# Routing whole rows: tokens, gates and routing values scattered by class, expert groups loaded plainly, results added into the output

## The reference, cut to what matters

```
logits = h3 @ Wg.T                        # 8 experts
val, idx = top_k(softmax(logits), 2); val /= val.sum() + 1e-9
out = 0
for e in range(8):
    a, b = split(h3 @ W1[e].T + b1[e], 2) # 2 x 256
    out += ((a * sigmoid(b)) @ Wo.T + bo) * comb[:, e]
result = x2 + gb * out                    # gb: one row of 128 for each sequence
```

## Time and profile before

| | us |
|---|---|
| median of three runs | 815.12 (813.99 to 816.86) |
| the profiled execution | 810.64 |
| its span | 808.8 |

### The profile page before, as it was taken

One profiled execution on the slowest core, in us unless ns is written; L12 is line 12 of the kernel. 1 busy time (PEld: TensorE's weight loads), 2 busy tenths in 40 slices (PEclk: granted clock), 3 DMA queues, 4 the chain that ended last, 5 costly groups with the idle time before them and its releaser, 6 DMA issues. The chain is left out here.

```text
span 808.8 us, 14121 instructions
## 1 busy us (share of the span) xinstructions
PE 669.2 (83%) x3703; PEld 521.4 (64%) x3703; DVE 657.2 (81%) x1426; ACT 474.8 (59%) x1163; POOL 613.5 (76%) x657
## 2 busy tenths in 40 slices
PE   2566899998999789988877967329879999999993
PEld 0444577676777558665655756118668888888882
DVE  5399999999999999979999467707748887788873
ACT  3664789887997678875655655214334444444441
POOL 5377878998998688999779785636777777777763
PEclk7798999999999899998999977559989999999997
DMA  4987767887887867766774262423144433333320
GB/s 125 244 129 139 125 142 132 130 161 131 157 157 125 127 114 133 128 110 115 100 95 94 63 171 64 95 63 84 32 107 104 97 92 95 97 97 96 97 65 1
DMA packets 95298, 89.64 MB, mean 111 GB/s; under 512 B 22832, under 2 KB 71194, under 8 KB 95094
## 3 DMA queue, kind: packets, MB, share of 16 engines
q1 hardware_dynamic: 84438, 66.49, 45.0%
q0 software_dynamic: 10784, 22.25, 9.9%
HBM read 38.69 MB, written 22.41 MB: 76 GB/s over the span
## 5 line engine op out<-in xcount | busy, mean ns | idle before, releaser
L708 POOL TENSOR_TENSOR rs_prod<-rT,state 128x512 f32<-128x512 f32 x128 | 165.2, 1303 | 35.9 <-DVE state L1287 34.0
L1743 POOL DMA_INDIRECT xg<-tokens_scratch,listed x91 | 88.9, 977 | 42.0 <-issue 25.6
L1749 POOL DMA_INDIRECT out<-res,listed x91 | 91.0, 1000 | 34.6 <-issue 25.7
L1282 DVE TENSOR_TENSOR kv<-key,v_spread 128x512 f32<-128x512 f32 x128 | 84.3, 669 | 10.6 <-DMA v_spread<-vT 9.3
L1713 ACT ACTIVATE sig<-ps_a 128x256 f32<-128x256 f32 x91 | 35.0, 385 | 82.5 <-PE ps_a L1653 69.1
L1287 DVE TENSOR_TENSOR_SCAN state<-decay,state,kv 128x512 f32<-128x512 f32 x64 | 79.9, 1269 | 0.1
L1287 DVE TENSOR_TENSOR_SCAN state<-decay,kv 128x512 f32<-128x512 f32 x64 | 76.0, 1207 | 0.1
L1067 PEld LDWEIGHTS ps_k<-w,gel 128*128 128x128 f32 x512 | 61.0, 199 | 14.7 <-issue 12.5
L1715 ACT ACTIVATE sig<-ps_b 128x256 f32<-128x256 f32 x91 | 35.0, 384 | 51.5 <-PE ps_b L1653 51.5
L1067 PE MATMUL ps_k<-w,gel 128*128 128x128 f32 x512 | 64.0, 285 | 1.2 <-ACT gel L924 1.2
L1790 DVE SCALAR_TENSOR_TENSOR ps_a<-ps_a,listed,sig 128x256 f32<-128x256 f32 x91 | 44.3, 487 | 24.8 <-ACT sig L1713 24.8
(11 more groups left out here) (298 smaller groups left out, 2068.4 us busy)
## 6 DMA issues: line engine op xcount, KB each, us to landing
v_spread<-vT SPq DMA_DIRECT2D x128, 256.0 KB, 6.5
xin<-in_L_attn_x SPq DMA_DIRECT2D x16, 256.0 KB, 7.2
tokens_scratch<-mods_scratch SPq DMA_DIRECT2D x16, 256.0 KB, 10.4
x<-in_L_attn_x SPq DMA_DIRECT2D x16, 256.0 KB, 4.8
tokens_scratch<-x SPq DMA_DIRECT2D x16, 256.0 KB, 5.4
tokens_scratch<-h SPq DMA_DIRECT2D x16, 256.0 KB, 4.5
list_scratch<-gel SPq DMA_DIRECT2D x1, 3584.0 KB, 11.9
rs_prod<-in_L_ffn_W SPq DMA_DIRECT2D x8, 256.0 KB, 5.3
```

The costliest lines, as they stand in the source:

```text
L708: pool.tensor_tensor(rs_prod[:, p, idx % 4], rT[p][:], state[idx][:, p * NT:(p + 1) * NT], ALU.mult).then_inc(s["rs_ready"], 1)
L1282: dve.tensor_tensor(kv[idx % 2][:], key[:], v_spread[idx % SPREADS][:], ALU.mult).then_inc(s["kv_ready"], 1)
L1743: pool.indirect_dma_start(xg[:, 2 * (k % LOADS) + i, :], None, pay_dram, bass.IndirectOffsetOnAxis(ap=listed[:, j, ID:ID + 1].bitcast(I32) ...
L1749: pool.indirect_dma_start(out_rows, bass.IndirectOffsetOnAxis(ap=listed[:, j, ID:ID + 1].bitcast(I32), axis=0), res[k % RESULTS][:, i, :], ...
```

## The change

A row of 260 values (1040 B) now carries everything of one token: `h3`, the gate row, and the four tags. `sorted_scratch` holds 28 classes with room for all tokens and 128 rows of slack each. It replaces both scratch tensors; `tokens_scratch` keeps only `h3` of twelve tiles.

- `x2` is stored to the output itself. In the expert block the scatter adds the result onto it (`compute_op=ALU.add`), so that DVE no longer adds `x2`: `gate` and `finish` become one multiplication.
- The clearing of the list goes. One block of 128 blank rows is stored at the start, and in the expert block 28 copies of that block, DRAM to DRAM, are put behind the ends of the classes (`fill_end`), after the first 12 group loads and before the rest. The late groups wait for them.
- For two of three listed batches SP stages pairs of groups (`stage_pair`: three DMAs, `h3` from DRAM, the gate row broadcast, the tags), two pairs in each iteration; POOL scatters them from there (`list_pair`). The third batch and the late four tiles lie in `last_rows`, which takes the place of the scan states when these are done; `load_last_rows` brings the third batch's tokens (1 MB) and four gate rows, broadcast (2 MB), in iteration 20 before SP's other work, and POOL scatters all 16 groups of it at one spot.
- The second batch's listings are spread like the first's (two at each odd spot) instead of being hurried.
- In the expert block SP loads each group's rows directly to `xg`; POOL only has the 16 late listings (four in each of the first four pairs, before the scatters) and the scatters.
- `out_w_rows` is loaded in `load_experts`; a copy of the classes' ends to `end_table` stands before the late table.

```diff
-                for t, p, b in tile(4):
-                    sp.dma_start(pay_gates[t], mods_dram[b, GB:GB + 1, :].broadcast_to([NT, P])).then_inc(s["gates_stored"], 16)
+                for r in batch(3):
+                    stage_pair(r, 0)
...
+            def stage_pair(r, m):
+                if r < LISTED - 1:
+                    first, k = r * RG + 2 * m, m % 2
+                    sp.wait_ge(s["route_step"], r * Router.STEPS + Router.TAGGED)
+                    for p in range(2):
+                        sp.wait_ge(s["h3_stored"][p], 16 * BATCH // 2 * (r + 1))
+                    if r > 0 or m >= 2:
+                        sp.wait_ge(s["listed"][k], 16 * 2 * (r * RG // 4 + m // 2))
+                    sp.dma_start(stage[k][:, :, 0:P], pay_groups[:, first:first + 2, :]).then_inc(s["staged"][k], 16)
+                    sp.dma_start(stage[k][:, :, GATE:TAGS], mods_dram[first * P // (TPB * NT), GB:GB + 1, :].unsqueeze(0).broadcast_to([P, 2, P])) \
+                        .then_inc(s["staged"][k], 16)
+                    sp.dma_start(stage[k][:, :, TAGS:], tags[:, first:first + 2, :]).then_inc(s["staged"][k], 16)
+            def load_last_rows():
+                sp.wait_ge(s["rs_ready"], TILES * DK)
+                for p in range(2):
+                    sp.wait_ge(s["h3_stored"][p], 16 * (early // 2))
+                sp.dma_start(last_rows[:, 0:RG, 0:P], pay_groups[:, (LISTED - 1) * RG:, :]).then_inc(s["last_staged"], 16)
+                for i in range(2 * BATCH // TPB):
+                    first = i * TPB * NQ
+                    sp.dma_start(last_rows[:, first:first + TPB * NQ, GATE:TAGS],
+                                 mods_dram[early // TPB - BATCH // TPB + i, GB:GB + 1, :].unsqueeze(0).broadcast_to([P, TPB * NQ, P])).then_inc(s["last_staged"], 16)
...
             def list_some(r, spot):
+                if r < LISTED - 1 and spot % 2 == 1 and spot <= RG + 1:
+                    list_pair(r, spot // 2 - 1)
+                if r == LISTED - 1 and spot == 7:
+                    pool.wait_ge(s["last_staged"], 16 * (1 + 2 * BATCH // TPB))
+                    pool.wait_ge(s["tags_set"], 1)
+                    pool.wait_ge(s["route_step"], LISTED * Router.STEPS)
+                    for m in range(RG // 2):
+                        list_pair(r, m)
...
+            def load_group(j):
+                k = j // 2
+                if k >= LOADS and j % 2 == 0:
+                    sp.wait_ge(s["stored"][(k - LOADS) % RESULTS], 16 * count_to(k - LOADS, RESULTS))
+                row = sp.value_load(row_table[0:1, j:j + 1], min_val=0, max_val=CLASSES * STRIDE)
+                sp.dma_start(xg[:, slot(j), :], sorted_dram[bass.ds(row, P), :]).then_inc(s["x_in"][k % LOADS], 16)
+            def fill_end(c):
+                row = sp.value_load(end_table[0:1, c:c + 1], min_val=0, max_val=CLASSES * STRIDE)
+                sp.dma_start(sorted_dram[bass.ds(row, P), :], sorted_dram[CLASSES * STRIDE:, :]).then_inc(s["filled"], 16)
+            for j in range(2 * LOADS):
+                load_group(j)
+                if j == 1:
+                    sp.dma_start(out_b[:], ins["L0_ffn_bo"].unsqueeze(0).broadcast_to([P, P])).then_inc(s["small_in"], 16)
+            for c in range(CLASSES):
+                fill_end(c)
+            for j in range(2 * LOADS, GROUPS):
+                if j == early_groups:
+                    sp.wait_ge(s["listed"], 16 * RG)
+                    sp.wait_ge(s["filled"], 16 * CLASSES)
+                load_group(j)
...
             for k in range(PAIRS):
-                if k + AHEAD < PAIRS:
-                    gather(k + AHEAD, 0)
+                if k < LIST_AT:
+                    list_late(RG * k // LIST_AT, RG * (k + 1) // LIST_AT)
                 if k >= 1:
                     scatter(k - 1, 0)
```

More of the change, by code:

```diff
@@ L33 @@
 GATE_MIN = 0.25
-ID, LOW, HIGH, BOTH = range(4)
+ID, LOW, HIGH, BOTH, TAG = range(5)
+GATE, TAGS, ROW = P, 2 * P, 2 * P + TAG
 PACK = 1 << 12
@@ L393, in attention_block @@
         mods_early, mods_late = sb("mods_early", [P, 2, 2, P]), sb("mods_late", [P, 2, 3, P])
-        out_w_rows = sb("out_w_rows", [P, out_w.shape[1] * P])
+        stage = [sb(f"stage{i}", [P, 2, ROW]) for i in range(2)]
         setup = rs_prod[0:NROWS, 0].rearrange("p a n -> p (a n)")
@@ L698, in list_some, with list_pair @@
-            def list_some(r, spot):
-                first, end = listed_by(r, spot - 1), listed_by(r, spot)
-                if first < end:
-                    pool.wait_ge(s["route_step"], (r + 1) * Router.STEPS)
-                    pool.wait_ge(s["list_cleared"], 32)
-                for n in range(first, end):
-                    list_group(r, n)
+            pool.memset(unlisted[:, TAGS + ID:TAGS + ID + 1].bitcast(I32), TILES * NT).then_inc(s["unlisted_ready"], 1)
+            def list_pair(r, m):
+                k = m % 2
+                if r < LISTED - 1:
+                    pool.wait_ge(s["staged"][k], 48 * (r * RG // 4 + m // 2 + 1))
+                    pool.wait_ge(s["route_step"], (r + 1) * Router.STEPS)
+                for n in range(2 * m, 2 * m + 2):
+                    g = r * RG + n
+                    if r < LISTED - 1:
+                        pool.indirect_dma_start(sorted_dram, bass.IndirectOffsetOnAxis(ap=dest[:, g:g + 1], axis=0), stage[k][:, n % 2, :], None).then_inc(s["listed"][k], 16)
+                    else:
+                        pool.indirect_dma_start(sorted_dram, bass.IndirectOffsetOnAxis(ap=dest[:, g:g + 1], axis=0), last_rows[:, n, :], None).then_inc(s["last_listed"], 16)
@@ L732, in step @@
                     products(7, p)
+                    beside(t, LAST, number_last)
                 for t, p, b in tile(8):
@@ L1608, in count_to, with slot, share_of @@
             return sum(members(j) for j in range(k % ring, k + 1, ring))
-        def quad_of(j):
-            return j // LISTS if j < early_groups else LATE_QUAD + (j - early_groups) // LISTS
-        def listed_to(c):
-            return 16 * sum(quads[i][1] for i in range(c % LISTS, c + 1, LISTS))
+        def slot(j):
+            return 2 * (j // 2 % LOADS) + j % 2
+        def share_of(j, which):
+            return xg[:, slot(j), TAGS + which:TAGS + which + 1]
         block = ctx.enter_context(nc.Block())
```

192 lines of the change are left out of this document (85 added, 107 removed).

## The result

The changed kernel takes 844.23 us (842.79 to 847.24, 4 runs) against 814.56 us: ratio 1.0379, 95% interval 1.0351 to 1.0407. It is 30 us slower; 811 was forecast, with a range of 798 to 835.

A forecast was written before the change was run, and what follows sets the result against it. No one engine bounds the whole: DVE sets attention, chained small steps the drain, PE the experts except where it starves. −1 + 0 − 1.8 − 1.4 − 0.4 = −4.6 us took the median 815.1 to 811; range 798 to 835.

The forecast's parts named there:

- Start: Kernel start: without the clearing, DVE's first norm of a later tile waits less; −1 us, between 0 and −2.
- Steady iterations: Steady pipeline: removed gate broadcasts gain nothing, extra POOL work is hidden, staging fits the slack; 0, with +3 as bound.
- Rival D: Steady iterations: staging delays spread loads beyond their slack, about 2 us in each of some five iterations; 821, chance 0.06.
- Last rows: Before the drain: 3 MB queued ahead take 12 us at 263 GB/s, expert weights still come in time; 0.
- Rival B: Last rows: 2 MB of gate broadcasts go at 40 GB/s, expert weights come at 513; +22, 833, chance 0.10.
- Drain: Drain: two listings fewer gain 2.5 us, third batch's listings end about when DVE would; −1.8 us net.
- Start of the experts: Handover to experts: list load, gather and turn become one load and turn, turn 0 at 534.5; −5.8 us.
- Fills: Expert block: 28 fills at 1.1 us hold SP, so PE idles 12.9 us before turn 6.
- A: Fills cost by piece, 1.6 us each, and all loads behind them wait; 13 us added, 824, chance 0.22.
- A': Fills cost by bytes, 3.3 us each, and the loads behind them wait; +60, 871, chance 0.05.
- C: SP issues fills faster, at 0.91 us each, so the stall is 5.3 us shorter; 804, chance 0.07.
- Steady experts: Expert pairs: PE's work unchanged, 0; at the end a saved addition gives −0.4, last scatter's landing up to +2.4.

The follow-up runs named there:

- e1: Kernel before with the eight scan states in one tile, 1025 values apart, as in the changed kernel; ratio 0.9941.
- e4: Changed kernel with four gate rows of 64 KB loaded and spread by DVE instead of broadcast by DMA; 823.01 us.
- e14: Kernel before with each scan state beginning 4 bytes later in its tile, a repeat of e2; 805.88 us against 812.37, ratio 0.9933.
- e3: Changed kernel with the scan states 1032 values apart instead of 1025; 857.45 us where the kernel before took 918.71.
- e11: Changed kernel with each fill as two DMAs of 64 rows, each with its own register read; 886.71 us.
- e2: Kernel before with each scan state beginning 4 bytes later in its tile; ratio 0.9885.
- e10: Changed kernel whose scatter stores instead of adding, leaving x2 out of the result; 855.99 us where the kernel before took 915.12.

## Why the prediction was wrong, step by step

- **What bounds the kernel: half right.** PE sets the experts: pairs stay 5.27 us apart. But "DVE was busy 252.3 of 255, so DVE waited for nothing there" took busy for work. Part of that time was DVE standing behind POOL.
- **Start, −1.** Not seen: the first `h3` store is at 149.97, before at 150.16. DVE's wait of 7.20 us for `xin` is gone, and one of 9.53 us for a spread load, before 1.84, stands in its place.
- **Steady iterations, 0.** Failed: −9.3. The place of the states, which the diff shows only as a slice of a tile, is a part of it that e1 shows alone (ratio 0.9941). By e1 to e4 and e14 it is some 4 us, and 3.9 the rest, perhaps the difference between the broadcasts that left and the staging that came; this split is an estimate. The bound of +3 covered only a loss. Rival D falls: past the 9.53 us at the start DVE waits 3.5 us in all for spread loads.
- **Last rows, "12 us at 263 GB/s: 0".** The step that failed most: it priced 2 MB by the expert weights' rate although the gate row's, 40 GB/s, had the same one-row source. Measured: 25.5 us for 2 MB, 82 GB/s, between the two. And the cover was looked for in the wrong place. The prediction asked only whether the expert weights behind the load come in time. The first thing behind it that anyone needed was a staged pair, for which POOL waits, and behind POOL all else; the next was `exp_w`, for which PE waits 23.36 us and which the prediction doesn't price. Rival B had the source and the size (+22), at a chance of 0.10, and its 513 for the first product of the weights came near the 509.26 measured, but the weights were not what the drain waited for. The drain lost 35.2 in the first pair of profiles; e4 is 31.5 us shorter there than the changed kernel's first profile and 27.5 shorter than e3 on its own chip.
- **Drain, −1.8.** The two listings less are not to be seen under this. Without the broadcasts (e4) the drain is 3.7 us longer than before, and POOL waits 14.0 us for staged pairs: "where the change adds a wait, what is queued behind it" was asked of SP and not of POOL. To the first load it is 3.3 longer, not 0.6. The prediction had counted the 16 listings behind the last `h`; they took 21.6 us, not 20.3, and their rows of 1040 B landed 5.1 us behind the issue (the median of that stretch), not the 2.4 that it took from a scatter of 512 B. DVE's last table value ends 22.6 us behind the last `h`, as before (22.4), so it is by all signs the listings that the block's end now waits for.
- **Start of the experts, −5.8.** Right: −5.4, turn 0 is 4.4 us behind the first load.
- **Fills, a stall of 12.9 us.** Right in place, kind and releaser, too small in size: 19.9. A fill takes SP 1.32 us, not the 1.1 of a list load, which makes 6.2 of the 7.0 us, and lies just at the 1.3 from which the prediction had called the change slower than before. Rivals A and A' fall: the load behind the 28 fills lands in 3.2 us, and e11's half fills cost nearly as much as whole ones. C falls with the 1.32.
- **Steady experts, 0, and tail, −0.4 with +2.4 as bound.** Pairs as forecast. The last scatter is 8.1 us from the end before and 9.3 after, and comes 0.7 later behind the last turn: +1.9 from the last turn on.
- **The sum.** +36.6 where −4.6 was forecast, by the two profiles: 37.6 of the 41 are the drain, 6.7 the fills' size, 2.7 the stretch to the first load, 1.9 the tail, 0.4 the handover; the start and steady gain takes 8.3 back. In the medians it is 844.23 against a forecast of 811. The range ended at 835 because B (833) and a longer stall (A, 824) were each thought of alone.

## What to carry to other kernels

A bulk load put ahead of a queue must be priced by a row with the same source pattern, and its victims are found by walking the queue behind it instruction by instruction, through each engine that waits in order, not by asking for the one user that comes to mind. A broadcast of one DRAM row to a large tile was here better loaded once and copied by an engine that had time. Many small register-addressed DMAs cost their issue, so they go where that queue is idle, in pieces between the loads that someone needs.

## What the runs showed of the hardware that was not expected

- A POOL product of two 128x512 operands takes 1.09 us or 1.30, by where its second operand begins (period 16 bytes); 4 or 8 bytes behind the start of a tile is fast, 0 or 12 slow (all at 4: mean of 1100 ns in e2; all at 0: 1303).
- DVE's busy time contains waits behind POOL: 0.29 us of work shown as 4.07, and 5.5 us of 268 went when only POOL's products became shorter (e2, another chip).
- Four DMAs of 512 KB that each read one DRAM row 1024 times hold SP for 25.5 us, 82 GB/s; from distinct rows the same 2 MB take 10.6 us of SP's time instead of 24.4.
- A scatter that adds costs POOL 1557 ns, one that stores 1000 (983 in e10).
- A DRAM-to-DRAM copy of 128 rows of 1040 B costs SP 1.32 us with its register read, half of it 1.30 (e11).
- Between chips the kernel before differs by 13% (811 to 919 us), the changed one far less (843, and near copies 856 and 857). The cause is open.
